# Another hand-written order of the work items in a fused attention and mixture-of-experts layer

## The reference

```python
x = layernorm(x + attn(x, x, x, sa_*, causal=True), ln1)          # self attention, 1024 keys
x = layernorm(x + attn(x, ctx, ctx, ca_*, causal=False), ln2)     # cross attention, 77 keys
x = layernorm(x + moe(x), ln3)
# moe: router softmax over 8 experts, the 2 best of each token, softmax of their two weights,
# h = gelu(x @ w1[e] + b1[e])  (256 -> 1024), y = h @ w2[e] + b2[e]  (1024 -> 256), weighted sum
```

## Time and profile before

| | us |
|---|---|
| median of three runs (lowest, highest) | 792.84 (791.93, 794.49) |
| the profiled execution itself | 792.84 |
| its span | 791.1 |
| PE busy | 740.1 (94%) |
| PE weight loads busy | 504.9 (64%) |
| DVE busy | 402.5 (51%) |
| ACT busy | 380.0 (48%) |
| POOL busy | 238.3 (30%) |

### The profile page before, as it was taken

One profiled execution on the slowest core, in us unless ns is written; L12 is line 12 of the kernel. 1 busy time (PEld: TensorE's weight loads), 2 busy tenths in 40 slices (PEclk: granted clock), 3 DMA queues, 4 the chain that ended last, 5 costly groups with the idle time before them and its releaser, 6 DMA issues. The chain is left out here.

```text
span 791.1 us, 14690 instructions
## 1 busy us (share of the span) xinstructions
PE 740.1 (94%) x5275; PEld 504.9 (64%) x5275; DVE 402.5 (51%) x974; ACT 380.0 (48%) x776; POOL 238.3 (30%) x432
## 2 busy tenths in 40 slices
PE   6889999999999999999997799996999999999983
PEld 4444544555455545545663677895899999999931
DVE  4577777767666777565677453664111011011125
ACT  3325456655656657587753456332433333433303
POOL 8313400112353322424643153202222222222115
PEclk9999999999999999999997899998999999999998
DMA  8968200702046112323227826568699999999663
GB/s 273 289 163 233 83 1 4 201 3 83 1 121 203 49 19 59 106 74 109 56 109 243 263 89 237 179 215 299 187 322 336 331 318 321 344 323 316 200 209 124
DMA packets 95152, 140.29 MB, mean 177 GB/s; under 512 B 11855, under 2 KB 81077, under 8 KB 92597
## 3 DMA queue, kind: packets, MB, share of 16 engines
q1 hardware_dynamic: 78533, 109.95, 44.1%
q10 hardware_dynamic: 12896, 19.92, 7.4%
q0 software_dynamic: 3648, 9.45, 3.3%
HBM read 110.65 MB, written 28.65 MB: 176 GB/s over the span
## 5 line engine op out<-in xcount | busy, mean ns | idle before, releaser
L1450 DVE TENSOR_REDUCE neg_part_max<-work 128x1 f32<-128x512 f32 (+4 forms) x368 | 212.8, 625 | 79.1 <-PE work L906 40.0
L1220 ACT ACTIVATE arena<-score_pair 128x1024 f32<-128x1024 f32 (+2 forms) x224 | 179.8, 839 | 86.6 <-PE score_pair L939 51.0
L906 PE MATMUL work<-arena 96*128 96x77 bf16 (+4 forms) x640 | 119.2, 280 | 9.1 <-DVE neg_part_max L1450 3.0
L936 PE MATMUL score_pair<-arena 99*128 99x512 bf16 (+2 forms) x448 | 113.4, 336 | 0.0
L959 PE MATMUL out_acc<-arena 128*32 128x512 f32 (+4 forms) x896 | 107.3, 517 | 0.6 <-ACT arena L1232 0.5
L829 PE MATMUL score_pair<-arena 128*128 128x256 f32 x432 | 97.6, 379 | 0.0
L1380 DVE TENSOR_TENSOR arena<-score_pair,arena 128x256 f32<-128x256 f32 x27 | 11.5, 425 | 166.8 <-PE score_pair L829 164.2
L906 PEld LDWEIGHTS work<-arena 96*128 96x128 bf16 x640 | 49.8, 100 | 72.6 <-issue 35.4
L1860 POOL DMA_INDIRECT chosen_scratch<-arena,scatter_rows x36 | 35.5, 986 | 186.4 <-DVE arena L1382 183.6
L829 PEld LDWEIGHTS score_pair<-arena 128*128 128x128 f32 x432 | 80.1, 190 | 9.8
L823 PE MATMUL work<-arena 128*128 128x128 f32 x704 | 84.7, 279 | 0.5 <-ACT arena L1153 0.5
(11 more groups left out here) (263 smaller groups left out, 928.7 us busy)
## 6 DMA issues: line engine op xcount, KB each, us to landing
arena<-in_L_xattn_e_w SPq DMA_DIRECT2D x54, 1024.0 KB, 6.2
arena<-parts_scratch SPq DMA_DIRECT2D x24, 768.0 KB, 6.1
arena<-in_L_xattn_e_w ACTq DMA_DIRECT2D x18, 1024.0 KB, 5.8
parts_scratch<-arena_more SPq DMA_DIRECT2D x24, 384.0 KB, 3.2
parts_scratch<-arena_more SPq DMA_DIRECT2D x24, 256.0 KB, 3.4
arena<-chosen_scratch SPq DMA_DIRECT2D x16, 256.0 KB, 5.8
parts_scratch<-arena_more SPq DMA_DIRECT2D x24, 128.0 KB, 3.4
residual<-in_x SPq DMA_DIRECT2D x4, 512.0 KB, 7.9
```

What stands on the lines that cost most here:

```text
L906: m = pe.matmul(bank[:, j * it.w:(j + 1) * it.w], qa[st.half(it.g)][0:R_S, h, n0:n0 + P], k, start=True, stop=not it.last)
L936: m = pe.matmul(st2[pair][0:rows, j, 0:w], k, qa[st.half(it.g)][0:R_M, h, skip:QG], start=True, stop=not diagonal)
L1220: act_e.activation(pt[buf][0:rows, :, 0:w], st2[pair][0:rows, :, 0:w], ACT.Exp, scale=float(HD) ** -0.5).then_inc(pair_taken[pair], 1)
L1450: dve.tensor_reduce(pm[:, it.at, it.t, it.h0:it.h0 + it.nh], bank[:, 0:it.nh * it.w].rearrange("p (j k) -> p j k", j=it.nh), AX.X, ALU.max ...
```

## The change

Only the string `ORDER` changes. Every item is there before and after, with the same instructions; their places in the plan differ, and with them the bank that each banked item gets. The whole diff:

```diff
--- before.py
+++ after.py
@@ -252,17 +252,17 @@
 }
 
 ORDER = (
-    "x6prbspxrvxcvpsprlrcp2rm6rsvm4xm2xm4sxm3lmxm3vm2gymsm2sm6lm2pm2q2rm4pm2q2m2rpm2wm2prsm2wqm3qxqm3qxm5wqxm2qm3"
-    "smwlxqsmuqm2pm2wm2gqrm3wiyqm2prm2sq2wm3qwudmq2m2wsm2qmqm2wm2q2m2wm2q2m2wmq2m3wm2rqmqwm2q2dwqjqm2wmuq2mgmwymq"
-    "m3q2mdwmqmqm2wmq2m3wqm2qm2wq2m3wqm2qwqm3wuq2mpm2qwm3q2lrmwm2qwsmq2m2qmgplwuqm2qmywmqmvm2wmdq2m2wqm2q2m2wuvmd"
-    "qmqmdwm2q2m2wt2qm3qwqm2wm2q2m2qmgywm2q2motwrm3q2wq2m3wqmuo2twmq2m2wm2qmqomqmp2m2wq2m3wqmsm2eawaq2m3wq2m2wmq2"
-    "ma2rqm2wuvx2q2m2smwxq2m3wq2lxwmsmgmq2wd2upm2wm2yq2rdmpmrvm2q2m2wmq2m2wt2wum3q2otqrm2qmwslsm2qwsmqmotmq2o2pwg"
-    "ym2q2m3wqm3qmwpmq2eam3wq2mwqm2rlqwum2aq2md2wqm2wvam2q2m2wsmqn2qmwn2qm2rsqnwmxmq2n2wnq2m3wxq2mwuhyqaxqm3wqvm2"
-    "q2m2wq2wxdqmwm2uqlqmprdwuqm3q2sn2wum2gq2n2lwq2n3wq2nhdyw2duidynt2po2t2q2no2qwq2un3wurnqdqndsqneaha2wt2q2lwyx"
-    "2q2axnwxqn2qpnrpwn2q2wn2slrothq2pwq2yw2urqotosqoqwuq2dwupqsdqedwuan3qa3dnwnq2un2dRwrst2MqnlqototoRqoRqMwRMq2"
-    "MhnHywq2n2ea2wqPnKn2qa2wqn2wR2qShMRMq2wMwuRqMdyvzHqwut2PovotKtqoqoSdFeaq2wuqawuBdxa2kqwux2OIA2xAXDdp2ANAdrsr"
-    "sNU3WVUln3Nn2tn3otNhlAtn3yn5oto2hyAq2eaYZqwuq2a3U2YU2Zdwuq2AYwuqZNdwuR2dNdMRtMAtMototoRoMHU2Yea4UNYZR2PKZL2R"
-    "2UNSL2CHUYZPKSUNU2TEYU2OzIA2XDYWZ2AYZ"
+    "x7prsbpxrsvcpcprpr2pvlm6svm2s2m14glm2im3ymrslm3pm4pm2q2m8rqwm2xqmqm3rqwqmxm3wmqxm4wmq2um2vm2xmxmxmqm2qmwm2q2"
+    "m3gwq2xm3w2ympmpsdsmqr2m3luqm2qm2qm2wm2q2msmwmqmqmgmwm2q2m2wm2wmqm2qmqmwqm2qswqxmqm2qmwuqm2qmwqm2qmwm2qmwymq"
+    "mqm2wm2q2m3wm2q2d2wq2m2prmpm2wq2m2wumpm2qm3q2jmwqmlm2wgq2m3qwqm2qmwusyqmqm2wmdq2mwqm3qwr2q2m2wupdpdq2mwvm2q2"
+    "m2ws2ltmqrm2qwtgm2q2m2wm3q2m2wyq2m3wqmqwmwuqm2qo2t2q2m3wqmdmwmq2om2qwq2m2ovm2rwm2q2m3wq2eam2smwq2m2a2w2m2q2m"
+    "uvm2q2mpmwq2x2amwmdsqwmrmq2x2qwm2gprlprum2q2m2smwytq2sm3wtwmq2mdotwuq2smdotlwmlmq2m2o2prspq2m3wqm2qmwmgemwmq"
+    "2rmnvm2q2nmwsqnm2qwnq2m2a2wqnmqnmwumq2nmwmyqnqmhmwm2q2m3wm2qmqmwymq2m2amwqm2qawm2wq2x3qm2qmdwxqlqum2pm2wq2m2"
+    "vwmq2m2wqmwmrmquprd2q2m2wumq2mwumn2q2gwslsnqn2qnwnq2ndyw2unhvd2yitntoto2tnq2oq2lwqunqen2wun2qdqdwq2hytawa2qx"
+    "qwn2tqnqn2wqawnx2qoxq2n2prswqwqhypq2otwtrlqupqo2srewuq2dwusdqpwuq2dwudqn2wn3a3q2an2drswR2t2nq2M2ototqoR2qMho"
+    "wlnMq2nenwn2q2HnwPa4Kq2n2RSwRq2M2w2uR2MdvMHt2yotPoKtohyqSqwuoedFq3vwuqwua3Bq2xawx2dzdudxOIAtXtDp2roNsANrsU3W"
+    "VA2lnln4Nn3ot2hnyn4Unoq2n2koYhyea2wuq2aAdA2YR2wuNAaZ2Mq2RMRq2M2HUwuPUdwuNd2U2AYtU2YtototoNoNU2Z2KSeaYUaRa2zY"
+    "RZLRLRNL2CUNHPKSTZU2YU2EOIA3XY2Z2DZW"
 )
```

## The result

| kernel | median, us | lowest to highest | runs | ratio, 95% interval |
|---|---|---|---|---|
| before | 792.88 | 791.09 to 796.59 | 10 | |
| after | 798.66 | 793.82 to 802.64 | 10 | 1.0064 [1.0037, 1.0092] |

The change costs 5.8 us between the medians. I had forecast a gain of 8.

A forecast was written before the change was run, and what follows sets the result against it. PE was almost always busy in the long stages, leaving 5.4 us of idle there; the holes to win were elsewhere. 792.84 - 7.0 + 0.5 - 2.5 + 1.5 = 785.3, given as 785 us, range 778 to 790.5.

The forecast's parts named there:

- The end of the plan: At `t_down8`: `experts` behind `t_down6` gives w2 a head start over w1, ending PE's wait; 7.0 us gained.
- The list of signs: At the end: `t_down8` waits under 2 us, w2 lands within 7, SP's first w1 is issued 2 or more behind.
- the reckoning that with the wait the low clock goes too: At `t_down8`: without its wait it runs at full clock, 3.72 us instead of 5.32.
- rival (a): At `t_up` 9: w1, gathered tokens or the clock hold it back; term 3 instead of 7, 789 us; chance 0.11.
- its bound, 8.3: Largest gain allowed at the end of the plan, 8.3 us, if neither added cost (0.8 and 0.5 us) is paid.
- What I priced at 0.8 us of loss: Behind `t_down8`: ACT's part of `w_diff` now stands ahead of ACT's copy for tile 9, costing 0.8 us.
- 402 to 464: Stretch at 402 to 464 us with 10 us of PE idle: earlier weights, stores and loads, 2.5 us gained.
- The beginning up to 402: From the start to 402 us: less PE work among the maxima of s0, partly recovered; 1.5 us lost.
- The sign named in the forecast: The maxima of s0 end with 4 us less PE work done at about the same time.
- part comes back: By 402 us DVE, 70% busy from 87 on, recovers part of up to 4 us lost; 1.5 us stays lost.
- Routing: 464 to 532 us: a new 0.9 us wait at the last `c_prefix`, other moves even; cost 0.5 us.
- (c): Self attention becomes bound by DVE because maxima stand denser; slower, 795 us at 96% PE busy; chance 0.07.

The follow-up runs named there:

- h3: Kernel before with `experts` behind `t_down6`, and `t_weights` moved ahead of both exponentials of s7 g0 q1: 787.58 us, ratio 0.9938 against before.
- e3: Kernel after with `t_weights` moved behind both `score` of s7 g0 q1: 795.13 us, ratio 1.0025 against before.
- f3: Kernel before with items 905 to 1062 (routing of the first half, `t_weights`, `rows`, loads of s6 and s7) in after's order: 800.38 us, ratio 1.0098.

## Why the prediction failed

- **The end of the plan** (-7.0): right in place and mechanism, and in size up to `t_down8`, -7.0 in the part. The list of signs held: `t_down8` doesn't wait, w2 lands in 5.5 us, SP is 1.95 us behind. The Trainium skill (DMA: Bandwidth & Descriptors, Queues, rings and completion order) says that a DMA engine takes turns between queues a packet at a time; in after the two queues meet only when most of w2 has moved, it has its engines alone at first, and it lands at the shortest time of the earlier trace rows. Wrong was the reckoning that with the wait the low clock goes too: it came behind the turn instead, at `t_up` 9, for 1.7 us, as rival (a) had allowed for. Without it the term would have been its bound, 8.3: `t_up` 9 starts 15.1 us behind `t_up8` instead of 23.4. What I priced at 0.8 us of loss, ACT's part of `w_diff` behind `t_down8`, was by the profiles a gain of about 2, because DVE's `w_split` had been in the way of tile 9 all along, hidden under the wait for w2. I asked what a removed wait uncovers on SP and DMA, and not on DVE.
- **402 to 464** (-2.5, bounds -5 to +2): measured +5.5 by lateness, +6.6 to +7.4 by time, outside the bounds. This is the failed step. Its sum valued each moved item by the cover it gives and put the routing of the first half, `t_up1b` and what follows the first maximum at nothing. The stores and loads of s6 did go out sooner against the projections, by 2.7 and 0.8 us (I had said 1), but `t_up1b` had left their cover, so the first maximum is no less late. What the sum left out cost 3.4 us in small waits before `t_weights`, from 384 us on, and 2.0 us behind the first maximum of s6. That is read from profiles; the moves behind each were not singled out. `t_weights`, which I suspected after the result, costs 0.3 us alone in the order of before (h3), with intervals of 2 us on either side. In after's order, moved behind both exponentials, it gave 3.5 (e3), so its share there stays open.
- **The beginning up to 402** (+1.5, bounds -2.4 to +6): +4.8 for the beginning. The sign named in the forecast came true (by the same sums of work, about 4 us less PE work done at the last maximum of s0, at 82.9 to 84.8 us against 81.4 to 85.7 in before's order), but the "part comes back" did not: none of the seven profiles with that beginning is less late at 339 us of PE work than at 67 by more than 0.2 us. The parameter rows of `v_bias`, which the forecast had landing "just about when DVE comes to it", at no cost, keep DVE waiting for up to 2.5 us. Another +1.3 is the loads of s2, a place that the forecast passed over with the remark that both orders had done the same by then. They had; the distance from s0's last weighing, which frees the buffers, to s2's first maximum had shrunk from 10 to 7 us of work.
- **Routing** (+0.5, bounds -2 to +2): +2.0, at the bound. The wait at `c_prefix` that I priced at 0.9 is 0.92 where it shows. The other moves from 464 to 532, which I took as even, less 0.4, cost the rest.
- **The rivals**: (c) had the right side, slower, and the wrong cause. DVE doesn't become the bound of the self attention; between 143 and 339 us of work the orders are equal to 0.1 us.

The terms with measured sizes: +4.8 + 1.3 + 5.5 + 2.0 - 7.0 - 1.5 - 0.1 = +5.0.

## What to carry to other kernels

A wait with a name in the profile can be priced; an order of more than a thousand items that is tuned against itself can't be priced by cover alone, and every place where it is shaken deserves a bound on the losing side as wide as the idle time already there. When one item is behind a gain, move that item alone: here one swap of two letters gives 5.6 us (787.26, the lowest median of all kernels measured), and the other moves take it away. A long wait in a list is not a loss by its length: the 4.83 and 4.38 us of after stand where before has other waits or more work, and most of what `rows` lost lay in waits under 1 us that compare only when the same work is laid side by side. And when a wait goes, look on every engine for what had been hiding under it.

## What the runs showed of the hardware

- The same order starts differently from one execution to the next: up to 67 us of PE work, twelve profiles with before's order spread over 4.7 us (-4.3 to +0.4), and in most of them lateness then stays as it is for 270 us. In the beginning PE's clock was low for 0 to 10 us in them.
- A hole costs again behind it. Kernels with the late w2 had a second stretch of 3 to 4 us at 1.2 GHz in the loop, 3 us behind the first, in three of five profiles, and lost 2.5 to 3.0 us from `t_down8` on against the profile of before; the two without it (before and f3) lost nothing.
- A head start decides who gets the DMA engines. w2 (1 MB) issued 0.07 us behind the first of two w1 on the other queue landed in 12.8 us, SP's queue moving 1.23 MB and ACT's 0.28 in 4 us; issued 1.95 us ahead of them it landed in 5.5.
